# Splitting the merged matrix and the first features beside the experts' first twelve tiles, and four landing places for the first batch's gathers

## The reference, cut to what matters

```python
# layer 0: a mixture of 16 experts, two for each of the 2048 rows
w = zeros((rows, 16)).at[rows, top2].set(normalised probabilities)
h = silu(x @ g.T) * (x @ u.T)                      # 112 columns per expert
x = x + tanh(g_ffn[0]) * einsum('bei,hei,be->bh', h, d, w)
# layer 1: attention over ctx
xn = layernorm(x)
Q = xn @ Wq.T + bq ; K = ctx @ Wk.T + bk
x = x + tanh(g_xattn[1]) * softmax(Q @ K.T / 32) @ ctx
```

## Time and profile before

| | |
|---|---|
| median of 3 runs | 1417.61 us (1416.63 to 1420.79) |
| profiled execution | 1419.29 us, of which the span from the first to the last instruction is 1417.6 us |
| granted TensorE clock, mean | 0.969 of full |
| experts | about 553 to 872 us of the span, the tiles from 616 to 868 |
| context_attention | from 872.6 us on |

### The profile page before, as it was taken

How to read it: one execution, slowest core, us unless ns; L and a number is a source line. 1 busy time by engine, 2 the same in 40 slices (tenths; PEclk the granted TensorE clock), 3 DMA queues, 4 the chain that set the end, 5 groups by cost and what they waited for, 6 DMA issues and landing times. The chain is left out here.

```text
span 1417.6 us, 21035 instructions
## 1 busy us (share of the span) xinstructions
PE 1267.5 (89%) x6498; PEld 860.6 (61%) x6498; DVE 786.1 (55%) x2006; ACT 550.9 (39%) x913; POOL 579.5 (41%) x960
## 2 busy tenths in 40 slices
PE   3799999999976999999999994999999999658786
PEld 1354545445444854468777883888888889335443
DVE  2878888887863670023333333644554433449995
ACT  2544444444423400024343444232222232068884
POOL 4776868676732000012221222623222221157885
PEclk9999999999988999999999997999999999979999
DMA  5210212302003503038778865325323330121111
GB/s 192 78 71 30 89 59 94 128 30 104 0 1 139 221 1 125 21 95 260 253 224 260 270 211 192 119 91 133 106 90 120 120 90 31 59 68 45 59 59 74
DMA packets 52479, 156.36 MB, mean 110 GB/s; under 512 B 5952, under 2 KB 16192, under 8 KB 52288
## 3 DMA queue, kind: packets, MB, share of 16 engines
q1 hardware_dynamic: 39152, 113.60, 22.5%
q0 software_dynamic: 13264, 41.95, 10.7%
HBM read 113.06 MB, written 45.61 MB: 112 GB/s over the span
## 5 line engine op out<-in xcount | busy, mean ns | idle before, releaser
L1163 PEld LDWEIGHTS ex_bank<-ex_xT,ex_gu 128*112 128x112 f32 x1248 | 140.3, 177 | 25.2 <-issue 24.3
L1163 PE MATMUL ex_bank<-ex_xT,ex_gu 128*112 128x128 f32 x1248 | 144.0, 274 | 2.1 <-issue 1.0
L44 PE MATMUL xa_bank<-xa_fT_high,M_hi 128*128 128x256 f32 x512 | 145.6, 284 | 0.0
L45 PE MATMUL xa_bank<-xa_fT_low,M_hi 128*128 128x256 f32 x512 | 144.9, 283 | 0.0
L46 PE MATMUL xa_bank<-xa_fT_high,M_lo 128*128 128x256 f32 x512 | 144.9, 283 | 0.0
L52 PE MATMUL la_bank<-la_osum,la_tab 128*128 128x512 f32 x256 | 121.0, 618 | 15.8 <-POOL la_osum L297 14.6
L297 POOL TENSOR_TENSOR la_osum<-la_oprod 128x512 f32<-128x512 f32 x64 | 80.1, 1274 | 96.8 <-DVE la_oprod L476 96.8
L1051 POOL TENSOR_TENSOR ex_small<-listed,ex_small 128x1 int32<-128x1 int32 x42 | 8.0, 190 | 236.6 <-DVE Wk L1118 236.5
L1402 DVE SCALAR_TENSOR_TENSOR X<-ffn_row,weights,X 128x1024 f32<-128x1024 f32 x32 | 48.6, 1517 | 93.0 <-DMA ffn_row<-produced,xa_small_u 92.7
L44 PEld LDWEIGHTS xa_bank<-xa_fT_high,M_hi 128*128 128x128 f32 x512 | 98.4, 192 | 0.3
L45 PEld LDWEIGHTS xa_bank<-xa_fT_low,M_hi 128*128 128x128 f32 x512 | 98.4, 192 | 0.0
(11 more groups left out here) (278 smaller groups left out, 2907.5 us busy)
## 6 DMA issues: line engine op xcount, KB each, us to landing
produced<-Wk SPq DMA_DIRECT2D x39, 512.0 KB
ex_gu<-in_gate_up SPq DMA_DIRECT2D x16, 896.0 KB, 6.5
X<-in_x SPq DMA_DIRECT2D x8, 1024.0 KB, 7.6
la_v_raw<-in_ctx SPq DMA_DIRECT2D x16, 512.0 KB, 4.0
produced<-la_zeros SPq DMA_DIRECT2D x16, 512.0 KB, 4.7
normal<-rt_xn SPq DMA_DIRECT2D x16, 512.0 KB, 5.6
xa_fT<-in_ctx_T SPq DMA_DIRECT2D x8, 1024.0 KB, 5.5
xa_f<-in_ctx SPq DMA_DIRECT2D x8, 1024.0 KB, 4.9
```

Of the source, the lines that this page charges most:

```text
L44: pe.matmul(out, a[0], b[0], start=first, stop=False)
L45: pe.matmul(out, a[0], b[1], start=False, stop=False)
L1163: m = pe.matmul(bank[half][0:INTER, 0:P], gu[:, slot, at:at + INTER], xT[:, k, :], start=(k == 0), stop=(k == KD - 1))
```

## The change

1. `merged_high`, `merged_low` and the first features' two halves leave `context_attention`. In `experts` the first `BESIDE` = 12 tiles of ACT's and DVE's loops are written out; the hardware loop runs from 12 on. Tiles 0 to 7 carry one column block of `M_hi` on ACT and of `M_lo` on DVE each, tiles 8 to 11 one of four parts of `fT_high` and `fT_low`. All `M_lo` blocks are DVE's now.
2. The load of the first `fT` moves into `experts`, on SP's queue behind the first three experts' weights, after a wait for the merged product.
3. `fT`, its halves, `xn` and `xT` lie in the home of Wk, which stays allocated.
4. The first batch's four gathers have four address slots and four places (`got` twice, `xn` twice), wait for no combine, and stand ahead of the memsets on POOL. DVE does `row_low(0)` before the four combines.
5. PE waits at the start for neither `consts` nor `ones` nor halves: `row_term(0)` is first, `consts` is waited for in `turn`, `ones` in `scores`.

```diff
 # experts
+            sp.wait_ge(s["m_pe"], 2 * KD - EARLY)
+            sp.dma_start(fT[:], features_T[0:1].rearrange("o (k p) t -> p (o k) t", p=P)).then_inc(s["fT_in"], 16)
             for e in range(EXPERTS):
...
-            with act.Fori(0, total) as g:
+            def tile(g):
                 act.wait_ge(s["gate_done"], g + 1)
                 act.activation(sg[:], bank[0][0:INTER, 0:P], ACT.Silu).then_inc(s["silu_done"], 1)
                 rows_out(g + 1)
+                if isinstance(g, int) and g < KD:
+                    part = merged_columns(g)
+                    act.activation(M[0][part], M32[part], ACT.Copy).then_inc(s["m_hi"], 1)
+                elif isinstance(g, int):
+                    part = features_part(g - KD)
+                    act.wait_ge(s["fT_in"], 16)
+                    act.activation(fT_parts[0][part], fT[part], ACT.Copy).then_inc(s["fT_hi"], 1)
                 act.wait_ge(s["down_done"], g + 1)
                 act.wait_ge(s["y_st"], 16 * g + 16)
                 act.activation(y[:, 0:512], bank[4][:], ACT.Copy).then_inc(s["y_act"], 1)
+            act.wait_ge(s["m_out"], 2 * KD - EARLY)
+            for g in range(BESIDE):
+                tile(g)
+            with act.Fori(BESIDE, total) as g:
+                tile(g)
...
 # DVE's tile, likewise written out twelve times
                 rows_out(g + 1)
                 hold(g + 2)
+                if isinstance(g, int) and g < KD:
+                    part = merged_columns(g)
+                    dve.wait_ge(s["m_hi"], g + 1)
+                    dve.tensor_tensor(M[1][part], M32[part], M[0][part].bitcast(F32), ALU.subtract)
+                elif isinstance(g, int):
+                    part = features_part(g - KD)
+                    dve.wait_ge(s["fT_hi"], g - KD + 1)
+                    dve.tensor_tensor(fT_parts[1][part], fT[part], fT_parts[0][part].bitcast(F32), ALU.subtract)
                 dve.wait_ge(s["down_done"], g + 1)
...
 # context_attention
-            load_turned(0)
             load_rows(0)
...
-                at_least(pool, s["combined"], n - 1)
+                if b > 0:
+                    pool.wait_ge(s["combined"], i + 1 if b == 1 and i < 2 else n - 1)
...
-            gather(0, 0)
-            gather(0, 1)
+            for i in range(4):
+                gather(0, i)
...
-            gather(0, 2)
-            gather(0, 3)
-            for m in range(POOL_LOW, KD):
-                merged_low(pool, m).then_inc(s["m_lo_pool"], 1)
             gather(1, 0)
...
-            for m in range(3):
-                merged_high(m)
             act.wait_ge(s["gate_in"], 32)
...
-            merged_high(3)
-            features_high(0)
-            for m in range(4, KD):
-                merged_high(m)
...
-            for m in range(3):
-                merged_low(dve, m).then_inc(s["m_lo"], 1)
-            combine(0, 0)
-            merged_low(dve, 3).then_inc(s["m_lo"], 1)
-            features_low(0)
-            combine(0, 1)
-            merged_low(dve, 4).then_inc(s["m_lo"], 1)
-            combine(0, 2)
-            combine(0, 3)
             row_low(0)
+            for i in range(4):
+                combine(0, i)
...
-            pe.wait_ge(s["consts"], 1)
-            pe.wait_ge(s["ones"], 1)
...
                 pe.wait_ge(s["row_lo"], b + 1)
+                pe.wait_ge(s["consts"], 1)
...
-                pe.wait_ge(s["fT_lo"], 4 * b + 4)
-                if b == 0:
-                    pe.wait_ge(s["m_lo"], min(m + 1, POOL_LOW))
-                    at_least(pe, s["m_lo_pool"], m + 1 - POOL_LOW)
+                at_least(pe, s["fT_lo"], 4 * b)
```

More of the change, by code:

```diff
@@ L977, in _, with experts @@
                 merged_product(pe, bank[n % 4][:], W, n).then_inc(s["m_pe"], 1)
-def experts(nc, gate_up, down, normal, listed, produced, first_tile, W, M32):
+def experts(nc, gate_up, down, normal, listed, produced, first_tile, W, M32, M, features_T, fT, fT_parts):
     with ExitStack() as ctx:
@@ L1004, in experts @@
         names = """one consts current rows_ready rows_held turned xT_act xT_dve gate_done up_half up_done silu_done hT_ready down_done
-                   m_pe m_out y_act y_dve y_st all_stored""".split()
+                   m_pe m_out m_hi fT_in fT_hi y_act y_dve y_st all_stored""".split()
         s = {n: sem(n) for n in names}
@@ L1124, in _, with tile @@
             total = dve.value_load(first_tile[0:1, EXPERTS:EXPERTS + 1], min_val=1, max_val=MAX_TILES)
-            with dve.Fori(0, total) as g:
+            def tile(g):
                 dve.wait_ge(s["silu_done"], g + 1)
@@ L1134, in _ @@
                 dve.tensor_copy(y[:, 512:1024], bank[5][:]).then_inc(s["y_dve"], 1)
+            for g in range(BESIDE):
+                tile(g)
+            with dve.Fori(BESIDE, total) as g:
+                tile(g)
         @block.tensor
@@ L1177, with context_attention @@
 SCORE_SCALE = float(D) ** -0.5
-def context_attention(nc, produced, slots, weights, ffn_gate, features, features_T, M32, M, shift, key_bias, constant, gate, X,
-                      after, ffn):
+def context_attention(nc, produced, slots, weights, ffn_gate, features, features_T, M, shift, key_bias, constant, gate, X,
+                      after, ffn, xn, xT, fT, fT_parts):
     with ExitStack() as ctx:
@@ L1204, in context_attention @@
         row_gate = weights[:].rearrange("p t k -> p (t k)")
[L1205 to L1209, removed]
-        G = sb("G", [P, KD, L])
[L1211 to L1215, removed]
+        small_u = sb("small_u", [P, 6], U32)
+        at = [small_u[:, i:i + 1] for i in range(4)]
+        spare, nought = (small_u[:, i:i + 1] for i in (4, 5))
+        G = sb("G", [P, KD, L])
         f = sb("f", [P, 2, D])
@@ L1225, in context_attention @@
         names = """gate_in consts one tg_done xn_ready turned xT_act xT_dve g_pe g_out s_pe maxed exped p_turned pT_out
-                   out_pe added nought at combined row_gate row_pe row_hi row_lo ones m_hi m_lo m_lo_pool fT_in fT_hi fT_lo f_in chain gains""".split()
+                   out_pe added nought at combined row_gate row_pe row_hi row_lo ones fT_in fT_hi fT_lo f_in chain gains""".split()
         s = {n: sem(n) for n in names}
         arrived = [sem(f"arrived{i}") for i in range(2)]
+        arrived_first = [sem(f"arrived_first{i}") for i in range(2)]
         block = ctx.enter_context(nc.Block())
@@ L1232, in context_attention, with landing @@
         row_bank = bank[7][0:2, 0:L]
[L1233 to L1241, removed]
+        def landing(b, i):
+            return xn[:, i - 2, :] if b == 0 and i >= 2 else got[i % 2][:]
         @block.sync
@@ L1312, in _ @@
         def _(act):
-            def merged_high(m):
-                part = merged_columns(m)
-                act.activation(M[0][part], M32[part], ACT.Copy).then_inc(s["m_hi"], 1)
             def features_high(b):
-                act.wait_ge(s["fT_in"], 16 * (b + 1))
+                act.wait_ge(s["fT_in"], 16 * b)
                 for i in range(4):
```

43 lines of the change are left out of this document (29 added, 14 removed).

## The result

| | before | after |
|---|---|---|
| median | 1417.38 us (4 runs, 1416.63 to 1420.79) | 1396.43 us (4 runs, 1391.36 to 1397.26) |
| ratio, 95% interval | | 0.984 [0.9812, 0.9869] |
| profiled execution, span | 1419.29, 1417.6 us | 1396.99, 1395.3 us |
| granted clock, mean | 0.969 | 0.970 |

A forecast was written before the change was run, and what follows sets the result against it. PE was taken as the bound in tiles and attention, idle only at the boundary between them. 15.4 (boundary) + 2.4 (table loads) = 17.8 us off the median 1417.6 gave 1399.8 us, range 1396.5 to 1406.

The forecast's parts named there:

- The boundary: Start of the attention block: PE begins at 872.8 instead of 888.2, saving 15.4 us; first matmuls still at half clock.
- The rows: First attention batch: normalised rows ready at 896.5, PE wants them at 899.4; 3 us of slack, no charge.
- the rows are late next: Rival, first batch: consts, gathers or norm hold the turn up to 4.9 us, or PE starts late; 1403.8 us, chance 0.15.
- The halves in the tiles: First twelve expert tiles: the added ACT and DVE work is covered and costs 0, at most 23.5 us without cover.
- the other side: Rival, first twelve tiles: halves come in series with y and cost the whole 23.5 us; 1423.3 us, slower, chance 0.03.
- DVE and POOL collide: Rival, tiles: shared port delays gathers or stretches DVE, y late in eight tiles, 5 us; 1404.8 us, chance 0.10.
- The table loads: First twelve tiles: one silu table load instead of one per tile ends four waits for hT, saving 2.4 us.
- tiles 1 to 11 none: Written-out expert tiles: one silu table load in the first tile, none in the other eleven.
- Everything after is PE's and shifts: Attention after the first batch's start: PE's work only moves earlier, with no change in its length.

The follow-up runs named there:

- peel_one: The kernel before with only the first turn of ACT's tile loop written out, no half moved: 1414.8 us, ratio 0.9981.
- pad64_before: The kernel before with an unused array of 64 bytes per partition ahead of the feature halves: 1408.4 us, ratio 0.9942.
- pad64_after: The kernel after with 64 unused bytes ahead of the home of Wk, so the feature halves lie at 32 modulo 128 again: 1395.6 us, ratio 0.9858.
- peel_and_pad: The kernel before with ACT's first tile written out and 64 unused bytes ahead of the feature halves: 1409.3 us, ratio 0.9931.
- after_third: The kernel after, unchanged, run a third time on the chip of its group: 1396.7 us, ratio 0.9849.
- two_places: The kernel after with the first batch's gathers as before the change, two places instead of four: 1398.7 us, ratio 0.9854.

## Why the prediction was right, and where it fell short

**The boundary** was right in mechanism and size: 15.4 us forecast, 15.4 between the means. PE began in the first tenth of a microsecond of the block, at the low end of its bound, and the first matmuls ran at the half clock, 3.4 us for `row_term`, as before.

**The rows** were right in outcome: no wait, four places needed. The rows were 1.3 us early for a forecast 3, so the rival *the rows are late next* was near: with two landing places PE waits 3.0 us.

**The halves in the tiles** cost nothing that shows, as forecast. The rival *the other side* fails on its price: with the whole chain made serial it was 6 to 9 us, so the kernel would still have been faster, 1400.9. The rival *DVE and POOL collide* had its mechanism right (190 to 366 ns) and no one waits for that operation.

**The table loads** were near in size, 2.4 forecast against 2.8 between the trace means and 1.1 and 2.6 in the timed pairs, and wrong in scope. That the size fits is luck: two errors met. The step read "tiles 1 to 11 none" and left one in each of the 27 looped tiles. It counted only the four stalls of the first twelve tiles, and gave back each of them in full. In fact the loads went from all 39 tiles, with 3.5 and 6.2 us of waits of PE for hT in the two traces of before, and about half of that reached the time. The loop needs no load once it is entered with silu's table: before, nothing ahead of the loop had loaded that table, and the load stood inside it. peel_one shows it with a single tile written out. The Trainium skill ("ScalarE activation tables: per-element evaluation and per-set limits", Table sets in the compiler and the runtime) says that loads are placed per block by longest run. By a rule that every block begins with a load, the 39 would have stayed; the trace has one.

**The step that failed** is the one that read "Everything after is PE's and shifts". The stretch from `row_term(0)` to the last output product was counted at no change and took 5.9 us less. Its 1536 G products went from 120 ns to 113 and 118 each, and item 3 of the change had moved `fT_high` and `fT_low` from 32 to 96 beyond a multiple of 128. In the traces they took 185.2 us before and 180.4 after, so 4.8 less: 0.62 in each of the seven later batches, and the rest in batch 0, part of which ran at the half clock. The other 1.1 of the 5.9 us is the half clock near the end of the stage, which two of the three traces of after did not have. I had taken item 3 as naming where things lie and priced nothing for it. pad64_before, with no instruction changed, shows that it has a price, and pad64_after gives back 3.3 of the 4.8; what the other 1.5 hang on is open. With the 4.8 the sum would have been 17.8 + 4.8 = 22.6, and the medians' 21.0 lies between the two. That the miss of the range is only 0.07 us says little, since repeats of the kernel after gave medians of 1394.4 and 1396.7.

The parts do not add up exactly in the timed medians. From peel_and_pad to after_third it is 12.6 us, where the boundary alone is 15.2 to 15.6 in the traces; the difference of the two ratios is uncertain by about 3.8 us (the root of the sum of squares of their half intervals), and peel_and_pad's six runs spread over 10 us.

## What to carry to other kernels

When a change moves an array that TensorE reads, compare the step from one matmul to the next in an untouched stretch before saying that the stretch only shifts; an unused array of 64 bytes ahead of it is a cheap test. It was worth 9 us on the kernel before. On the kernel after, where it puts the halves back, it cost nothing that the time shows, so it has to be tried on the kernel that is kept. Before a hardware loop in which ScalarE alternates a table function and copies, run that function once, so that the loop is entered with its table. Hiding work beside a bound engine is worth what the waits absorb, and a loss of cover must be priced by what reaches that engine: 6 to 9 us here, not the sum of the durations, 23.5.

## What the runs showed of the hardware

- The step of back-to-back matmuls of 256 columns in 32-bit floats at full granted clock was 120, 118 or 113 ns. With moving and stationary operands at 32 bytes beyond a multiple of 128 it was 119 to 120 in six traces; with the features at 96 beyond it was 113 or 118 in all eleven traces that had that; with them at 0 it was 118 to 121 in one, with a batch as long as at 32 (23.35 us). Duration alone hides it: the median duration at line 44 is 283 ns before and 276 in pad64_before, since the matmuls overlap.
- The same program gave batch 0 at 113 ns in one execution and at 118 in two others. Neither has been explained.
- ACT's table load took 1283 ns each time and silu started right behind it (624.46 + 1.28 = 625.74, start 625.75).
- PE began a block 0.04 us after POOL, after 5.7 us of idling.
- Waiting 3.0 us in two_places, PE was granted half the clock (0.50) for 10.2 us around the end of the wait.
